# Patch tokens of a ViT tower, taken chunk by chunk: 128-column passes, copies three chunks later, and a first row without the shifted columns

## The reference

```
patches = X.reshape(B, 3, 8, 28, 8, 28).transpose(0, 2, 4, 1, 3, 5).reshape(B, 64, 2352)
tokens  = einsum('bpi,hi->bph', patches, W) + b          # W: 128 x 2352
h = concat([class_token, tokens]) * pos_embed            # B x 65 x 128
h = h + gated_attention(layernorm(h))                    # per image position: EMA, QK, values, gate, layernorm
logits = layernorm(h).reshape(N, 128) @ Wr               # N = 128 * 65, 8 experts
probs  = softmax(logits, axis=0); vals, idx = top_k(probs.T, 1024)
out    = h + scatter_add(vals * (gelu(x[idx] @ W1 + b1) @ W2 + b2))
```

## Time and profile before

| | us |
|---|---|
| median of three runs | 998.42 |
| profiled execution | 988.4 |
| its span | 986.6 |
| TensorE busy, share of the span | 756.6, 77% |
| DVE, POOL, ACT busy | 556.1, 477.7, 446.5 |
| passes (L1352), both MATMULs of each | 313.2 |
| DMA share of the 40 slices, first 22 | 0.8 to 0.9 and more |

### The profile page before, as it was taken

The page is one execution under the profiler, slowest core; times in us unless marked ns, Lnnn a source line. Parts: engine busy times, 40 slices in busy tenths (PEclk is TensorE's granted clock), DMA queues, the critical chain, the costliest instruction groups (busy, mean ns, idle before and its releaser), DMA issues.

```text
span 986.6 us, 9758 instructions
## 1 busy us (share of the span) xinstructions
PE 756.6 (77%) x2896; PEld 396.9 (40%) x2896; DVE 556.1 (56%) x1238; ACT 446.5 (45%) x730; POOL 477.7 (48%) x488
## 2 busy tenths in 40 slices
PE   0168489999999999999999995625128899788771
PEld 0123235544544554454445543414114455344330
DVE  0210157778778877877787777592687543231110
ACT  0634357656665775666566522321253132222220
POOL 2233444555545554645555322261110768888885
PEclk9778789999999999999999996856556799899896
DMA  9699998898889889888988111000010233343432
GB/s 224 155 207 212 199 208 203 195 217 192 207 196 218 195 206 218 198 191 200 217 191 197 49 31 34 21 12 11 22 14 1 47 53 63 63 66 63 66 38 27
DMA packets 135681, 126.39 MB, mean 128 GB/s; under 512 B 17605, under 2 KB 126013, under 8 KB 135501
## 3 DMA queue, kind: packets, MB, share of 16 engines
q1 hardware_dynamic: 113600, 91.27, 40.1%
q0 software_dynamic: 19488, 33.51, 18.0%
q10 hardware_dynamic: 2540, 0.99, 0.5%
HBM read 87.99 MB, written 12.98 MB: 102 GB/s over the span
## 4 chain that ended last, share of the span: by engine, by line
PE 25%; DVE 24%; POOL 20%; issue 15%; DMA 8%; ACT 5%; SPq 2%; ACTq 1%; DVEq 0%; POOLq 0%
PE bank L1352 10%; POOL out L620 9%; POOL XS L610 6%; DMA XS<-in_x 5%; DVE Y L966 4%; PE bank L1450 3%; DVE stats L916 3%; DVE O L908 3%; DVE XR L908 2%; DVE QT L1041 2%; ACT XS L819 2%; POOL rsB L492 2%; PE bank L1435 2%; PE bank L1481 2%; SPq L421 2%
## 5 line engine op out<-in xcount | busy, mean ns | idle before, releaser
L1352 PE MATMUL bank<-XS,WT 126*128 126x512 f32 (+1 forms) x608 | 313.2, 651 | 33.9 <-DMA XS<-XS 33.9
L801 ACT ACTIVATE XS<-XS 84x1152 f32<-84x1152 f32 (+1 forms) x192 | 187.6, 1027 | 34.7 <-DMA XS<-in_x 32.5
L1352 PEld LDWEIGHTS bank<-XS,WT 126*128 126x128 f32 (+1 forms) x608 | 113.2, 195 | 169.7 <-issue 168.8
L567 POOL COPY XS<-XS 84x1152 f32<-84x1152 f32 x64 | 89.0, 1390 | 82.1 <-DMA XS<-in_x 79.1
L620 POOL DMA_INDIRECT out<-XS x64 | 103.3, 1614 | 26.6 <-issue 18.6
L580 POOL DMA_DIRECT2D XS<-XS x128 | 71.3, 560 | 56.0 <-PE bank L1352 41.1
L610 POOL DMA_INDIRECT XS<-token_rows,XS x64 | 65.0, 1016 | 47.8 <-DVE XS L1244 28.6
L966 DVE TENSOR_TENSOR_SCAN Y<-qdec,XT 128x512 f32<-128x512 f32 (+1 forms) x68 | 78.5, 1175 | 8.4 <-ACT XT L688 8.4
L848 ACT ACTIVATE XS<-bank,VT 128x512 f32<-128x512 f32 x64 | 44.0, 687 | 66.8 <-PE bank L1562 66.8
L1562 PE MATMUL bank<-XS 128*128 128x512 f32 x128 | 69.5, 693 | 1.4 <-ACT XS L688 0.8
L972 DVE SCALAR_TENSOR_TENSOR ET<-Y,ema_c,ET 128x512 f32<-128x512 f32 (+1 forms) x68 | 61.7, 907 | 1.8
(11 more groups left out here) (236 smaller groups left out, 1289.3 us busy)
## 6 DMA issues: line engine op xcount, KB each, us to landing
XS<-in_x SPq DMA_DIRECT2D x192, 392.0 KB
XS<-XS POOLq DMA_DIRECT2D x128, 189.0 KB, 7.6
out<-O SPq DMA_DIRECT2D x16, 256.0 KB, 6.7
token_rows<-XR SPq DMA_DIRECT2D x16, 256.0 KB, 6.9
XS<-in_L_ffn_W SPq DMA_DIRECT2D x16, 256.0 KB, 3.1
XS<-in_L_tok_W SPq DMA_DIRECT2D x1, 1176.0 KB, 9.3
XS<-token_rows,XS POOLq DMA_INDIRECT x65, 2.6
out<-XS POOLq DMA_INDIRECT x64
```

The costliest lines, as they stand in the source:

```text
L567: pool.tensor_copy(ST[0:ROWS, n % 2, :, :, :].rearrange("p m j r -> p m r j"), px[:, :, :, PASSES:PATCH])\
L801: ins = act.activation(area(slice(0, ROWS), k // 4, piece, m0, m0 + CCOL // 2).rearrange("p m j r -> p m r j"), px[:, :, :, REST * piece:m ...
L1352: ins = pe.matmul(TOK[half][:, :], WT[rows, t, :], area(rows, half, t // REST)[:, :, t % REST, :], start=(t == 0), stop=(t == PASSES - 1))
```

## The change

1. **Passes by chunk.** A pass takes the 128 columns of one chunk. `STREAM` lists all (chunk, t); `token_pass(p)` takes the next one. TensorE waits for the copy and the shift of that chunk alone, and counts `pe_tok` once for each chunk. The tables `FILL` and `FILL_CLS` now count these short passes.
2. **Copies three chunks later.** Slot (i, u) now copies chunks 8i+4u+1 to 8i+4u+4 (`chunk_of`), where it copied 8i+4u+4 to 8i+4u+7. Before the first slot three chunks are copied and not four, and `SLOT` has the copies at other places.
3. **Chunks 3 to 7 of the first row are direct** (`DIRECT`): they are not shifted. They take 28 passes each, all with 84 rows, the last nine straight from POOL's staging buffer `ST`, with weights that are transposed extra (`WQ`, `rest_weight`). So `ST` is free again only when the passes of the chunk are done.
4. **The start in another order.** ACT copies c0 before it moves anything out of PSUM, c1 before `WT`, c2 after it. DVE lays out W without the wait for `c_loaded`.

```diff
+        SLOT = ["S b", "C 0 3", "w 0", "T a", "U b", "C 0 0", "Z b", "P b", "N a", "K 0", "X a", "E a", "C 0 1", "C 0 2",
...
+        AHEAD = 3
+        DIRECT = range(3, CHUNKS)
...
+        def chunk_of(i, u, place):
+
+            if i == 0:
+                return AHEAD + 4 * u + place if 4 * u + place <= CHUNKS - AHEAD else CHUNKS * NP
+            return CHUNKS * i + 4 * u + 1 + place
...
-            for k in range(4):
-                stage_W(k, 0)
+            for n in range(AHEAD):
+                stage_W(n)
...
+            def stage_C(n, piece):
...
                 if begun(n - 2):
-                    pool.wait_ge(*extras[n % 2].done(n // 2 - 1))
+                    if n - 2 in DIRECT:
+                        pool.wait_ge(*pe_tok.done(n - 2))
+                    else:
+                        pool.wait_ge(*extras[n % 2].done(shifted(n - 2)))
...
+            def stage_w(n):
+
+                if n in DIRECT:
+                    return
...
+            first_copy(0)
+            evacuate(0, VT[:, :], bank[5][:, 0:120])
...
+            first_copy(1)
+            for n in range(4):
+                evacuate(3 + n, wt[0:KROWS, 512 * n:512 * n + 512], bank[n][0:KROWS, :])
...
             act.wait_ge(*c_loaded.done(0))
             act.activation(ema_t[:, 0:2, :], ema_in[:, 0:2, :], ACT.Exp, scale=-1.0).then_inc(pro_sig.sem, 1)
...
+            first_copy(2)
             act.wait_ge(*consts_done.done(0))
...
-            dve.wait_ge(*c_loaded.done(0))
             dve.wait_ge(*w_loaded.done(0))
...
+            STREAM = [(n, t) for n in range(CHUNKS * NP) for t in range(passes_of(n))]
...
                 if t == 0:
-                    pe.wait_ge(*copied.done(CHUNKS * i + 4 * half + 3))
-                    for k in range(2):
-                        pe.wait_ge(*extras[k].done(4 * i + 2 * half + 1))
-                    if begun(i - 1):
+                    pe.wait_ge(*copied.done(n))
+                    if n in DIRECT:
+                        pe.wait_ge(*staged.done(n))
+                    else:
+                        pe.wait_ge(*extras[n % 2].done(shifted(n)))
+                    if k % 4 == 0 and begun(i - 1):
                         pe.wait_ge(*dve_K[half].done(i - 1))
-                rows = slice(0, KROWS if t < 2 * REST else ROWS)
-                ins = pe.matmul(TOK[half][:, :], WT[rows, t, :], area(rows, half, t // REST)[:, :, t % REST, :],
-                                start=(t == 0), stop=(t == PASSES - 1))
+                rows = slice(0, KROWS if t < 2 * REST and n not in DIRECT else ROWS)
+                if t < PASSES:
+                    weights, pixels = WT[rows, t, :], area(rows, half, t // REST, m0, m0 + CCOL // 2)[:, :, t % REST, :]
+                else:
+                    weights, pixels = rest_weight(t - PASSES), ST[rows, n % 2, :, t - PASSES, :]
+                ins = pe.matmul(TOK[half][:, c0:c0 + CCOL], weights, pixels, start=(t == 0), stop=(t == passes_of(n) - 1))
...
-            FILL = {"T": 4, "P": 1, "V": 3, "L": 5, "D": 1, "I": 4, "Q": 1}
-            FILL_CLS = {"T": 4, "X": 4, "V": 6, "D": 2, "I": 2}
+            FILL = {"T": 15, "P": 4, "V": 13, "L": 20, "D": 4, "I": 16, "Q": 4}
+            FILL_CLS = {"T": 2, "X": 3, "V": 4, "D": 5, "I": 6}
...
+                end = passes_till(CHUNKS * i + 4 * u + (4 if i or u else 6))
+                if a is CLS and s in FILL_CLS:
+                    tokens_until(end, passes_till(FILL_CLS[s]))
```

More of the change, by code:

```diff
@@ L372, in slot @@
                 elif s in "CWw":
[L373 to L376, removed]
+                    n = chunk_of(i, u, int(w[0]))
+                    if tokens and n < CHUNKS * NP:
+                        keep.append((s, (n, *(int(v) for v in w[1:]))))
                 else:
@@ L385, in run, with iteration @@
         def run(eng, stages, tokens_at=None, last=True):
-            def iteration(i, slots, tokens, more):
+            def iteration(i, slots, tokens):
                 for u, (a, b) in enumerate(slots):
-                    for s, w in slot(i, u, a, b, tokens, more):
+                    for s, w in slot(i, u, a, b, tokens):
                         if s in stages:
@@ L662, in _, with stage_C @@
             act.dma_start(lnb[:, :], bass.AP(ln_b.tensor, 0, [[0, 128], [1, D]])).then_inc(c_loaded.sem, 16)
+            def stage_C(n, piece):
+                if piece == C:
+                    return
+                k = n % CHUNKS
+                if piece == 0:
+                    act.wait_ge(*load[n % RING].done(n // RING))
+                    if begun(n - CHUNKS):
+                        act.wait_ge(*pe_tok.done(n - CHUNKS))
+                px = RAW[0:ROWS, n % RING, :].rearrange("p (m r q) -> p m r q", r=2, q=PATCH)
+                m0 = CCOL // 2 * (k % 4)
+                ins = act.activation(
+                    area(slice(0, ROWS), k // 4, piece, m0, m0 + CCOL // 2).rearrange("p m j r -> p m r j"),
+                    px[:, :, :, REST * piece:min(REST * piece + REST, PASSES)], ACT.Copy)
+                if piece == C - 1:
+                    ins.then_inc(copied.sem, 1)
@@ new lines, in first_copy, with evacuate @@
+            def first_copy(n):
+                for piece in range(C):
+                    stage_C(n, piece)
+            def evacuate(n, dst, src):
+                act.wait_ge(*pe_pro.done(n))
+                act.activation(dst, src, ACT.Copy).then_inc(pro_evac.sem, 1)
+            wt = WT[:, :, :].rearrange("p t k -> p (t k)")
+            first_copy(0)
+            evacuate(0, VT[:, :], bank[5][:, 0:120])
+            evacuate(0, WvT[:, :], bank[5][:, 128:384])
+            evacuate(1, WmT[:, 0:4, :].rearrange("p k d -> p (k d)"), bank[6][:, :])
@@ L924, in stage_K @@
             def stage_K(half, hy):
-                dve.wait_ge(*pe_tok[half].done(hy))
+                dve.wait_ge(*pe_tok.done(CHUNKS * hy + 4 * half + 3))
                 dve.wait_ge(*pe_T.done(2 * hy))
@@ L1338, in _ @@
             pe.transpose(bank[4][0:ROWS, 256:384], WP[:, 18, 0:ROWS], ident[:, :]).then_inc(pe_pro.sem, 1)
+            pe.wait_ge(*c_loaded.done(0))
+            pe.wait_ge(*pro_evac.done(4))
+            pe.matmul(bank[7][:, 384:512], flip, relN, start=True, stop=True).then_inc(pe_pro.sem, 1)
+            pe.wait_ge(*pro_evac.done(2))
+            pe.wait_ge(*wq_ready.done(0))
+            for h, (b, j0, j1, c0) in enumerate(((5, 0, 4, 0), (6, 4, 8, 0), (2, 8, 9, 0))):
+                if b == 2:
+                    pe.wait_ge(*pro_evac.done(7))
+                for j in range(j0, j1):
+                    last = pe.transpose(bank[b][0:ROWS, c0 + 128 * (j - j0):c0 + 128 * (j - j0) + 128], WQ[:, j, 0:ROWS], ident[:, :])
+                last.then_inc(pe_pro.sem, 1)
```

136 lines of the change are left out of this document (58 added, 78 removed), and 6 rows, old and new, of the table SLOT.

## The result

The kernel after took 960.86 us in the median of four executions (959.49 to 961.95), the kernel before beside it 997.01 (995.05 to 999.37, four). The ratio is 0.9636, 95% interval [0.9608, 0.9664]: 36.2 us faster. The profiled execution took 960.5 us, 958.4 of them span.

The account below looks back on a forecast made before the run. The start waits for data, and TensorE sets the pace from 152.55 us. 988.4 - 25.5 - 1.0 + 2 + 1.5 = 965.4 for a profiled execution; with 10.0 carried over, a median of 975.5 us, range 967 to 991.

Parts of the forecast that it names:

- the 10 us: Whole kernel: timed median lies 10.0 us above the profiled execution, carried over from before to after.
- Row 1's first slot: First slot of row 1: 34.6 us against 35.6, with c9 and c10 loaded before it begins; 1.0 gained.
- Row 1's passes: End of the start: row 1's first pass at 91.5 us against 116.98, set by c8's shift; 25.5 us gained.
- Middle and last slots: Slots after row 1's first: +0.15 us in each of 12, 2 us lost; last slot, now beside copies, 1.5 lost.
- A short pass: Every pass of 128 columns: 0.24 us, a quarter of a long one, the strided pixels' extra going with the columns.
- A: Rival, every pass: fixed step exposed, a short pass costs 0.32 us, start gains only 9.5, time 1056; chance 0.12.
- B: Rival, middle slots: a shift lands 1.0 us late in each of 14 slots, time 989.5; chance 0.13.
- C: Rival, every pass: short passes at 0.224 us, row 0 gains 3 more, slots 5.6, time about 967; chance 0.10.
- D: Rival, start: staging from ST stops the loads, c8 no earlier, no start gained; c6 5 us late gives 980; 0.03 with the unknown.

Follow-up runs that it names:

- short_only: Kernel before with every pass cut into four of 128 columns, waits, copies and order unchanged: 994.06 us, ratio 0.9998.
- pe_early: Kernel after, c0's passes waiting for fewer of ACT's copies out of PSUM and consts_done waited for only behind them: 953.15, 975.13, 975.57 and 979.60 us.
- pe_early_two: pe_early with only c3 and c4 direct, c5 to c7 shifted again: 955.03 us, ratio 0.9662.
- early_fill: pe_early with one FILL_CLS number changed (V from 4 to 5), putting 13 us of class-token filler passes first instead of 7: 957.44 us, ratio 0.9635.
- early_fill_none: early_fill with no direct chunk (DIRECT = ()): 962.73 us, ratio 0.9702.

## Why the prediction was wrong

The direction, the mechanism and the price of a short pass were right, and the gain was too small by 12.2 us up to T(8,0): 23.0 against 35.2. The rest of the 14.6 is that before's median came out at 997.01 and not 998.42 (1.4), and 1.0 in the part behind T(8,0) and the scatter. To carry the 10 us between before's profiled execution and its median over to after gave the right medians, but the reason wasn't known: after's profiled execution (960.5) lies at its median (960.86), and before's had neither of the two waits behind T(8,0) that after's has. From profile to profile the forecast was 965.4 against 960.5, and that nearness is luck: 12.2 us too little gained up to T(8,0), against 7.0 lost behind it in a part for which no change was forecast.

- *Row 1's first slot: the step that failed.* Forecast was 34.6, "1.0 gained"; it took 29.18, 6.4 gained. I sized it as a middle slot with a little less waiting. Two things in it stood in the trace. First, its group b is the class token, one tile and not four: L1503 takes 0.45 us there and 1.79 in a middle slot (91.79 to 92.24, 257.07 to 258.86); with L1495, L1510, L1513, L1520, L1527 and L1534, each taken from its start to the next in the two slots, that makes 4.4 us of the 4.7 by which the slot is shorter. Second, before's slot of 35.57, which has the same small group, held waste that the change takes away: the wait of 4.40 us for ET, and the low clock at its head, 5.51 us for four passes against 4.00. Together that is 5.9 of the 6.4 us gained. ACT's timeline of before shows that wait's cause:

```profile
136.38 2.49 ACT L801 ACTIVATE XS<-XS 84x1152 f32<-84x1152 f32 x2 [4.14 <-DMA XS<-in_x]
138.74 0.62 ACT L717 ACTIVATE ET<-ET 128x512 f32<-128x512 f32 x1
```

  F, the writer of ET, stands behind a copy whose load is late. In after:

```profile
99.74 2.86 ACT L697 ACTIVATE XS<-XS 84x1152 f32<-84x1152 f32 x3
103.53 0.63 ACT L762 ACTIVATE ET<-ET 128x512 f32<-128x512 f32 x1 [0.93 <-DVE ET L999]
```

  the copies wait for nothing, F for DVE alone. All kernels in the old order had this slot at 35.6 to 37.0 (short_only too), all in the new at 29.2 to 32.7, whatever their first row was.

- *Row 1's passes: right step, terms too large.* 86.62 and not 91.5, 4.9 us. The first pass came 1.3 earlier (33.30: DVE's constants began at 28.04, not 29.2); c0 took 6.86 and not 7.5; T and X took 0.11 each, where I had 0.4 and 0.3, and V, D, I 0.45 each, where I had 0.6 and twice 0.8. Together c6 was done at 77.6 and not at 81.0. c8's copy, issue and landing took 9.0 us for my 10.2.
- *Middle and last slots: the sum had the right sign, the middle slots didn't lose.* 3.5 us lost forecast, 1.6 lost (438.94 to 440.51). Eleven slots from row 1's second on take together 0.1 us less than before, where +0.15 each was forecast: in the one shown PE is busy 0.1 us more, and its three gaps are 0.41, 0.34 and 0.41 us where they were 0.68, 0.32 and 0.36. The loss stands in the last two slots, 33.29 to 33.89 us and 31.74 to 32.83. short_only says the same of the short passes by themselves: no change that 0.15% would show.
- *A short pass: right.* 0.24. By Part 3 of the Trainium skill's "TensorE: Matmul & The Clock Gate" each short pass would show its weight loads; the 38 full loads of a chunk lie inside 4.54 us of 38 MATMULs, so the rule doesn't hold for these. The Trainium skill's "SBUF — State Buffer" left a fixed step as the one way to read the strided pixels' extra; a fixed step would have made the pass 0.32 us, and it takes 0.24.
- *Rivals.* A (1056) is out by short_only. B: no middle slot waits for a shift. C has the nearest time, 967, from a cause that isn't there: its pass of 0.224 was not seen. D: c6 was not late.
- *The range.* It was built from the uncertain prices, pass and waits. The two large errors were in steps that I gave no bounds at all.

What stays open: how the 24.7 us of the new stream divide between waiting by chunk and the later copies; no kernel did one without the other.

## What to carry to other kernels

When a change removes the wait ahead of a stage, read what that stage's first pass through its loop was made of (waits, low clock, smaller tiles at the edge); it is not a middle iteration less a little. Cutting the 512 columns of these float32 passes in four cost nothing (short_only), and what it bought is that TensorE can wait in smaller pieces. A stretch that runs ahead of its inputs needs its filler placed ahead of the first instruction that can be late: one number in a table moved row 1's first pass from 106.23 to 83.37 us between the two profiles.

## What the runs showed of the hardware

- In pe_early's profile the granted clock was 0.50 behind a wait of 2.00 us and stood there through nearly 50 us of 84-row passes (128 columns); it rose after 126-row passes had begun (0.50 from 106.2 to 110, 0.72 to 112, then 1.00), and did so too in pe_early_two. That the rows have to do with it isn't shown: 84-row passes ran for 34 us at 1.00 in after and in early_fill. Not each such wait has the effect: behind waits of 1.94 and 3.02 us in early_fill_none (73.19 and 80.99) the clock stayed at 1.00. The caveats in Part 1 of the Trainium skill's "TensorE: Matmul & The Clock Gate" warn that the clock's trace records can be unreliable and that the clock has been seen stuck for 50 us and more; here the durations say the same as the records, 0.43 us a pass and 72 MATMULs in 15 us instead of 126.
- Two waits of about 4 us each with no named releaser, in the last part of the kernel, stand in nine of the thirteen profiles and in none of the other four, whatever the kernel; before's median was 997.0, 994.6, 993.1 and 988.4 us in four jobs, the last of them on the chip where the profiles lack these waits. Profiles of two kernels should be compared up to a common instruction, and times within a job.
